# A Perceiver block on one core: the first chunk's differences and low parts on VectorE in another order, and clipping placed before the statistics in every chunk

## The reference, cut to what matters

```python
lat = layer_norm(latents, ln_lat_g, ln_lat_b)
ctx = layer_norm(context, ln_ctx_g, ln_ctx_b)      # context: (2, 2048, 512)
q = (lat @ Wq)...                                  # 16 heads of 64
k, v = jnp.split(ctx @ Wkv, 2, axis=-1)
k = apply_rope(k, cos[None, None], sin[None, None])
attn = jnp.einsum('bhnd,bhsd->bhns', q, k) * scale
attn = jax.nn.softmax(jnp.clip(attn, -11.0, 11.0), axis=-1)
out = jnp.einsum('bhns,bhsd->bhnd', attn, v) ... @ Wo + bo
```

## Time and profile before

| quantity | value |
|---|---|
| time, median of 3 runs | 1193.81 us (1192.96 to 1193.89) |
| profiled execution: time | 1195.95 us |
| profiled execution: span | 1194.2 us |
| TensorE busy | 1157.5 us, 97% |
| VectorE busy | 804.1 us, 67% |
| ScalarE busy | 543.1 us, 45% |
| GpSimd busy | 243.2 us, 20% |
| mean granted TensorE clock | 0.989 of full |

### The profile page before, as it was taken

The page is one execution under the profiler, slowest core; times in us unless marked ns, Lnnn a source line. Parts: engine busy times, 40 slices in busy tenths (PEclk is TensorE's granted clock), DMA queues, the critical chain, the costliest instruction groups (busy, mean ns, idle before and its releaser), DMA issues.

```text
span 1194.2 us, 23534 instructions
## 1 busy us (share of the span) xinstructions
PE 1157.5 (97%) x9792; PEld 947.4 (79%) x9792; DVE 804.1 (67%) x1349; ACT 543.1 (45%) x896; POOL 243.2 (20%) x184
## 2 busy tenths in 40 slices
PE   7789999999999999999899999999999999999998
PEld 5578888788788888864546667888899999999997
DVE  4859595968696868566788885265765566566562
ACT  5333333324242424124369997373644544444441
POOL 3316262626253536350000000010000000000000
PEclk9899999999999999999999999999999999999999
DMA  8224141414041413265232324302545445445440
GB/s 316 104 92 158 39 157 38 158 36 160 18 154 38 156 37 120 87 244 211 110 138 90 125 107 178 142 1 78 221 161 211 161 192 211 157 194 207 158 162 18
DMA packets 37376, 159.61 MB, mean 134 GB/s; under 512 B 3739, under 2 KB 3995, under 8 KB 26788
## 3 DMA queue, kind: packets, MB, share of 16 engines
q1 hardware_dynamic: 37284, 158.29, 36.0%
HBM read 153.56 MB, written 4.72 MB: 133 GB/s over the span
## 4 chain that ended last, share of the span: by engine, by line
PE 47%; DVE 3%; issue 2%; ACT 2%; DMA 0%; DVEq 0%
PE mid_bk L57 10%; PE mid_bk L58 10%; PE mid_bk L59 10%; PE mid_bk L1236 5%; PE mid_bk L1281 2%; PE mid_bk L1251 2%; PE mid_bk L1207 2%; PE mid_bk L1126 2%; PE mid_bk L1271 1%; DMA w_raw<-in_w 0%; PE mid_bk L1380 0%; DVE mo_w_lo L1913 0%; DVE mo_w_lo L1919 0%; ACT sa_sc L1546 0%; DVE x_sc L1827 0%
## 5 line engine op out<-in xcount | busy, mean ns | idle before, releaser
L645 POOL TENSOR_TENSOR norm_both<-norm_both,prob 128x512 f32<-128x512 f32 x118 | 166.0, 1407 | 89.0 <-DVE prob L417 81.6
L57 PE MATMUL mid_bk<-mo_x_hi,mo_w_hi 128*128 128x256 f32 x496 | 141.0, 284 | 0.0
L58 PE MATMUL mid_bk<-mo_x_lo,mo_w_hi 128*128 128x256 f32 x496 | 140.9, 284 | 0.0
L59 PE MATMUL mid_bk<-mo_x_hi,mo_w_lo 128*128 128x256 f32 x496 | 140.9, 284 | 0.0
L569 ACT ACTIVATE prob<-u_ps 128x512 f32<-128x512 f32 x128 | 66.1, 605 | 138.8 <-PE u_ps L795 138.8
L1919 DVE TENSOR_TENSOR mo_w_lo<-w_raw,mo_w_hi 128x2048 fp32r<-128x2048 f32 x32 | 73.3, 2292 | 73.0 <-ACT mo_w_hi L1628 73.0
L57 PE MATMUL k_ps<-ctx_hi,wk_hi 128*128 128x512 f32 x256 | 102.3, 400 | 0.8 <-ACT q_T L548 0.8
L1628 ACT ACTIVATE mo_w_hi<-w_raw 128x2048 fp32r<-128x2048 f32 x32 | 61.2, 1912 | 88.2 <-PE mid_bk L59 88.2
L57 PE MATMUL mid_bk<-mo_w_hi,mo_h_hi 128*128 128x512 f32 x256 | 100.2, 391 | 0.0
L58 PE MATMUL k_ps<-ctx_lo,wk_hi 128*128 128x512 f32 x256 | 100.2, 391 | 0.0
L58 PE MATMUL mid_bk<-mo_w_lo,mo_h_hi 128*128 128x512 f32 x256 | 99.9, 390 | 0.0
(11 more groups left out here) (279 smaller groups left out, 2485.3 us busy)
## 6 DMA issues: line engine op xcount, KB each, us to landing
w_raw<-in_w SPq DMA_DIRECT2D x64, 1024.0 KB, 6.0
wk_hi<-wk_parts SPq DMA_DIRECT2D x28, 512.0 KB, 4.2
wk_lo<-wk_parts SPq DMA_DIRECT2D x28, 512.0 KB, 5.1
ctx_raw<-in_ctx_rows SPq DMA_DIRECT2D x8, 1024.0 KB, 5.5
x_k<-in_ctx_T SPq DMA_DIRECT2D x8, 1024.0 KB, 7.3
x_val<-in_ctx_heads SPq DMA_DIRECT2D x8, 1024.0 KB, 4.8
tabs<-in_rot_tabs SPq DMA_DIRECT2D x8, 512.0 KB, 4.0
vals<-in_wq_rows SPq DMA_DIRECT2D x4, 512.0 KB, 8.0
```

The lines of the kernel that those rows point to most:

```text
L57: pe.matmul(out, w_hi, x_hi, start=start, stop=False)
L58: pe.matmul(out, w_hi, x_lo, start=False, stop=False)
L59: return pe.matmul(out, w_lo, x_hi, start=False, stop=stop)
L645: ins = pool.tensor_tensor(to, to, src, ALU.add)
```

## The change

At the start, GpSimd's work on the weights and on the first chunk's low parts goes to VectorE (`weight_sums`, `low_ctx`), in an order written out by hand up to turn 2. SyncE loads two quarters of Wq, then Wk, then Wv, and the other half of Wq and the table after them. ScalarE rounds Wk before the queries, and takes Wv in the order `w_order`, all ahead of turn 0. `low_k(3)` and `center(1)` move behind `turn_second(2)`, and `add_products(0, 0)` moves ahead of `clip(0)`. TensorE's waits follow: `project(0, a)` waits for one query copy less at a = 0, and the counts of `part_lo` are new. In every later chunk `stats(n + 1)` moves from ahead of `clip(t - 1)` to behind it, in the turns with r = 0.

```diff
-        NWD = 5
+        w_order = ("B11", "T2", "T3", "T1", "B21", "T4", "B22")
...
-            for g in range(NQ):
-                load_wq(g)
+            load_wq(0)
+            load_wq(1)
             load_wk(0)
             load_wk(1)
-            load_tab(0)
             for i, to in ((0, "B11"), (2, "T3"), (3, "B22"), (1, "B21")):
                 load_wv(i, w_of[to])
+            load_wq(2)
+            load_wq(3)
+            load_tab(0)
             load_ctx(1)
...
+            def low_ctx():
+                for k in range(KD):
+                    dve.wait_ge(s["cfull"], k + 1)
+                    dve.tensor_tensor(ctx_lo[:, 0, k, :], ctx_full[:, k, :], ctx_hi[:, 0, k, :],
+                                      ALU.subtract).then_inc(s["csplit"], 1)
...
             low_k(0)
             low_k(1)
-            for t in range(NT + 1):
+            weight_sums()
+            low_ctx()
+            sums(0)
+            for w in w_order[:4]:
+                low_v(w)
+            turn_first(0)
+            low_v(w_order[4])
+            turn_second(0)
+            low_s(0)
+            for w in w_order[5:]:
+                low_v(w)
+            low_k(2)
+            turn_first(1)
+            turn_second(1)
+            add_products(0, 0)
+            clip(0)
+            stats(dve, 1)
+            spread(dve, 1)
+            turn_first(2)
+            add_products(0, 1)
+            turn_second(2)
+            low_k(3)
+            center(dve, 1)
+            clip(1)
+            for t in range(3, NT + 1):
                 n, r = t // 4, t % 4
                 if t < NT:
-                    if t in (1, 2):
-                        low_k(t + 1)
                     if r == 2 and n + 1 < NC:
                         center(dve, n + 1)
                     turn_first(t)
                     if r == 2:
                         add_products(n, 1)
                     turn_second(t)
-                    if t == 0:
-                        sums(0)
                     if r == 3 and n + 1 < NC:
                         sums(n + 1)
                     if r == 0:
-                        if t == 0:
-                            for j in range(NWD):
-                                low_v(j)
                         low_s(n)
-                        if n + 1 < NC:
-                            stats(dve, n + 1)
-                if t >= 1:
-                    clip(t - 1)
+                clip(t - 1)
                 if t < NT:
                     if r == 0 and n + 1 < NC:
+                        stats(dve, n + 1)
                         spread(dve, n + 1)
...
             root(act, 0)
+            high_k(0)
+            high_k(1)
             queries(0)
             for k in range(KD):
                 context(0, k, k)
             queries(1)
-            high_k(0)
+            for w in w_order[:3]:
+                high_v(w)
             queries(2)
-            high_k(1)
-            high_v("B11")
-            high_v("B21")
+            high_v(w_order[3])
+            high_v(w_order[4])
             queries(3)
-            high_v("B22")
+            for w in w_order[5:]:
+                high_v(w)
...
-            for k in range(KD):
-                split(0, k)
-            weight_sums()
-            low_weights()
...
-                        pe.wait_ge(s["part_lo"], (1, 3, 4, 4)[bank])
-                    if bank == 1:
-                        pe.wait_ge(s["part_lo"], NWD + 2 * n + 2)
+                        pe.wait_ge(s["part_lo"], (1, 7, 7, 7)[bank])
+                    elif bank == 1:
+                        pe.wait_ge(s["part_lo"], NWB + 2 * n + 2)
...
-                    if t == 0:
-                        pe.wait_ge(s["q_out"], 4)
+                if t == 0:
+                    pe.wait_ge(s["q_out"], 3 + a)
```

More of the change, by code:

```diff
@@ L339, in _, with weight_sums, low_v @@
         def _(dve):
-            def low_v(j):
-                dve.wait_ge(s["part_hi"], j + 3 if j else 1)
-                dve.wait_ge(s["prepared"], (2, 3, 5, 5, 5)[j])
+            def weight_sums():
+                dve.wait_ge(s["wv_in"], 64)
+                for m, (dst, a, b) in enumerate((("T1", "T3", "B11"), ("T2", "B22", "T1"), ("T3", "B22", "T3"),
+                                                 ("T4", "B21", "T2"))):
+                    dst, a, b = (wv_raw[:, w_of[w], :, :] for w in (dst, a, b))
+                    dve.wait_ge(s["prepared"], m + 1)
+                    dve.tensor_tensor(dst, a, b, ALU.subtract).then_inc(s["prepared"], 1)
+            def low_ctx():
[3 more added lines that the diff above has]
+                                      ALU.subtract).then_inc(s["csplit"], 1)
+            def low_v(w):
+                j = w_of[w]
+                dve.wait_ge(s["part_hi"], w_order.index(w) + 1)
                 dve.tensor_tensor(wv_lo[:, j, :, :], wv_raw[:, j, :, :], wv_hi[:, j, :, :],
@@ L516, in high_v @@
                 if w in ("T1", "T2", "T3", "T4"):
-                    act.wait_ge(s["prepared"], 1 + int(w[1]) if w != "T3" else 4)
+                    act.wait_ge(s["prepared"], 1 + int(w[1]))
                 j = w_of[w]
@@ L598, in _ @@
                     high_k(t + 1)
-                if t == 0:
-                    for w in ("T1", "T2", "T3", "T4"):
-                        high_v(w)
                 if t < NT and r == 0:
@@ L749, in values @@
                 pe.wait_ge(s["v_kept"], 2 * v + 1)
-                pe.wait_ge(s["prepared"], 7)
                 product(n, ip, "A12", "B21", 0, False, True)
+                pe.wait_ge(s["part_lo"], NWB + 2)
                 pe.wait_ge(s["v_sum"], 5 * v + 2)
```

## The result

The changed kernel takes 1178.31 us (median of 4 runs, 1177.88 to 1178.94), the kernel before 1193.85: a ratio of 0.9866 with a 95% interval from 0.9847 to 0.9884. Forecast were 1176.4 us and a range of 1173 to 1181.5. The profiled execution took 1178.94 us.

What follows compares the result with a forecast made beforehand. TensorE is busy nearly throughout, so only its waits and half-clock time in the first cross attention can be won: 12.3 us in chunk 0 plus 5.1 later make 17.4, off the median 1193.81 gives 1176.4 us, range 1173 to 1181.5.

Steps and rivals of the forecast that it cites:

- The step from 86.15 to about 73.75: Start of chunk 1's transposes on TensorE: from 86.15 to 73.7 to 73.8, chunk 0 giving 12.3 us.
- The chain that the prediction wrote out for VectorE: First chunk: VectorE's new order timed step by step from Wv's landing at 18.95, letting values start at 43.3.
- The new wait ahead of the transposes: Before chunk 1's transposes: TensorE waits 2.0 us for `center(1)`, where it waited nothing.
- 5.1 us forecast: Later chunks of the first cross attention: 0.93 us in each of four chunks plus 1.4 in one; bounds 0 and 5.7.
- rival A: Later chunks: only the first chunk pays, additions still over L408 and L411 or VectorE bound at L378; 1181.3 us, 16%.
- the one with the bias additions: The later chunk with the wait of 1.7 us: gain 1.4, after about 0.5 of a new wait for L378.
- the slack at L394: Later chunks, second addition of the values (L378 before): ends at 182.2, TensorE wants it at 182.7.
- B: First chunk pays less: late Wv or Wq, missed `v_kept`, or half clock behind a short wait, each about 2; 1178.4 us, 14%.
- C: Slower: statistics contend with GpSimd at +1.09 us each, in the later chunks and at `v_kept` in chunk 0; 1203.1 us, 3%.
- B's other conditions: First chunk: Wv or Wq lands late, or `v_kept` misses its due time, each worth about 2 us.
- The forecast of 17.4 us: Whole kernel: gain of 12.3 us in chunk 0 plus 5.1 in the later chunks.
- the likeliest case: Whole kernel: the forecast itself, 1176.4 us with its own range of 1174.5 to 1178; chance 66%.

## Why the prediction was right

**The first chunk.** The step from 86.15 to about 73.75 was forecast and 74.01 measured. The chain that the prediction wrote out for VectorE fits within 0.3 us at each of these places: low context from 24.0 (measured 23.79), `sums(0)` from 26.4 (26.31), first turn from 33.8 (33.64), end of L378, now L394, 49.4 (49.12), end of `center(1)` 73.7 (73.95). Values start at 43.3 (43.45) and end at 52.8 (53.13). TensorE's granted clock is 1.00 through all of chunk 0, as forecast, where the kernel before had 0.50 in two stretches. The durations that carry it (1.15, 0.72 and 0.60 for work without GpSimd beside it) were those of rows where GpSimd was idle, and they hold. One term had no row: the weight sums stand in the chain at 5.0, 1.25 each, where the row gives 1.15. They measured 5.00. The new wait ahead of the transposes was put at 2.0 and is 1.86.

**An error that cancelled.** The prediction kept the first queries where they were. They ran faster in this execution: the transposes of chunk 0 start at 15.23 where they did at 16.72. That won nothing: 0.75 us went into a wait for the late half of Wq, which the prediction had arriving 0.5 us ahead of need, and the wait for `turn_first(0)` was 1.09 and not 0.6. The early start and the thin margin on Wq cancelled, which is luck. It is not the change either: the transposes of chunk 0 also start at 15.13 in the run with the old start and the new clip order. The chain stands on the landing of Wv. In the run with the new start only, the queries were late (transposes of chunk 0 at 17.31), and t1 still lies 55.13 us behind the first weight sum.

**The later chunks.** 5.1 us forecast, 4.8 to 5.0 measured, and rival A is out. The mechanism is as told: L427 at 0.68 us. A chunk won 0.98 to 1.00 us, in one case 0.86, where 0.93 was forecast, but the one with the bias additions won 0.98 and not 1.4: the wait for L394 that stays there is 0.9 and not 0.5. The size that was off is the slack at L394. The prediction had it at 0.5 us (182.7 against 182.2); measured are 0.1: L394 ends at 170.44, and the product after it is due at 170.31 + 0.23. So the forecast of this part held by 0.1 us. Part of the difference is `cva`, a tensor_scalar of 4 columns beside GpSimd's additions: 1.26 us where the forecast kept the old spread with 1.05. The run with the late additions, with 1.3 a chunk in place of 0.8, says the same.

**Rivals B and C.** C, the slower one, hung on statistics beside GpSimd. All 32 instances in the changed kernel take 0.668 to 0.695 us, those beside the additions too. The Trainium skill's page SBUF — State Buffer, "Who interferes with whom", by which a VectorE instruction with at most one SBUF input, outside the two-port modes, does not contend with GpSimd, agrees with these rows. B had TensorE fall to half clock behind a wait of 2.0 us. It did not: behind the 1.9 us the granted clock is 1.00 (us; busy time of TensorE, its weight loads, VectorE, ScalarE and GpSimd; granted clock; DMA share; GB/s):

```profile
72.00:74.00 2.00, 0.14 (x4) 0.00 (x0) 1.97 (x5) 0.33 (x1) 0.00 (x0) 1.00 0.64 262
74.00:80.00 6.00, 5.99 (x35) 5.27 (x36) 2.46 (x6) 5.30 (x8) 3.68 (x3) 1.00 0.69 247
```

It fell behind the 3.0 us of the run with the old loads (0.80 and 0.63), though not behind the 2.2 us of that run, and behind the 3.2 us of the one with the sums on GpSimd (0.56). The Trainium skill (TensorE: Matmul & The Clock Gate, Part 1) has the clock halved after an idle stretch; those two waits agree with it, and in the changed kernel it costs nothing. B's other conditions did not come either: the late half of Wq was there at 21.34, as forecast (21.4), and only the early queries met it; Wv and `v_kept` were in time.

**The total.** The forecast of 17.4 us fits the spans (17.0) and is 1.9 us off the medians (15.5, and 15.4 when repeated). The 1178.31 us lie within the whole range and 0.3 above the 1174.5 to 1178 of the likeliest case. The weak step is the last one of the sum: a gain worked out on one profiled execution was taken off the median. The execution profiled before was 2.1 us slower than its median, the one after 0.6 slower. Some of that was inside the change's own stretch: t1 is 85.61 in the kernel that has the old start and the new clip order, against 86.15. The rest of it was not traced to a place; the stretch behind t7, which no kernel here changes, varies from 742.3 to 748.8 us between executions. What share of the 1.5 us between the two measures comes from where stays open.

## What to carry to other kernels

When a wait is removed by moving work behind it, look at what the same engine delivers next: here the clip came 2.4 us earlier and would have won nothing, had the early clip not also moved GpSimd's additions off two instructions of VectorE. Splitting elementwise work with two SBUF operands between VectorE and GpSimd bought no time in either run that tried it (0.3 and 4.2 us later). Giving it to VectorE alone, in the order of need and behind loads in the same order, bought the 12 us of the first chunk. Taking back the load order costs 5.0 of them and the sums' engine 3.8; the remaining 3 or so, the order on VectorE and ScalarE above all, was not tested by itself. And with executions that differ by several us, compare landmarks inside the traces: read from the first weight sum, four executions of the same start agreed within 0.03 us, so that differences of 0.4 us could be told, which the medians could not.

## What the runs showed of the hardware

VectorE's 128x512 addition or subtraction with two SBUF operands goes from 0.72 us in a chain to 1.74 beside GpSimd (6.97 for 4), while statistics (at most 0.695 us) and operations with one of two operands in PSUM (0.68, L412) don't change beside GpSimd's additions; GpSimd is slowed as well (7.94 for four 128x512 where 5.28 was usual beside an idle VectorE). A tensor_scalar of 4 columns took 0.62 and 1.26 us in two places beside GpSimd's additions, and 0.17 alone. TensorE's granted clock stayed at 1.00 behind waits of 1.9 and 2.2 us and fell behind waits of 3.0 and 3.2 us. With the new load order Wv's landing moved by 1.2 us between executions (18.37 to 19.57 for the first weight sum), and the start of the kernel moved with it.
